# Scores, evictions and transposes in another order in a two-layer graph attention kernel on one core

## What is computed

```python
h = jnp.maximum(_layernorm(x), 0.0)
for l in range(2):
    m_left  = einsum('bsh,oh->bso', h, W_left[l]);  u_left  = einsum('bih,bjh->bij', h, m_left)  / sqrt(768)
    m_right = einsum('bsh,oh->bso', h, W_right[l]); u_right = einsum('bih,bjh->bij', h, m_right) / sqrt(768)
    u = u_left * triu(adj, 0) + u_right * swapaxes(triu(adj, 1), 1, 2)
    e = exp(u) * adj
    attention = e / (sum(e, axis=2, keepdims=True) + 1e-10)
    ctx = attention @ (einsum('bsh,oh->bso', h, W_lin[l]) + b_lin[l])
    h = relu(_layer_norm(ctx, ln_a[l], ln_b[l]))
return x + h
```

## Time and profile before

| | |
|---|---|
| median of 3 runs | 2853.18 us (2851.03 to 2854.72) |
| the profiled execution | 2853.21 us |
| its span, first to last instruction | 2851.4 us |
| TensorE matmuls busy | 2726.8 us, 96% of the span, 14400 matmuls |
| VectorE busy | 1658.9 us, 58% |
| ScalarE busy | 699.5 us, 25% |
| GpSimd busy | 109.2 us, 4% |
| DMA | 207.97 MB, mean 73 GB/s |
| mean granted TensorE clock | 0.994 |

### The profile page before, as it was taken

How to read it: one execution, slowest core, us unless ns; L and a number is a source line. 1 busy time by engine, 2 the same in 40 slices (tenths; PEclk the granted TensorE clock), 3 DMA queues, 4 the chain that set the end, 5 groups by cost and what they waited for, 6 DMA issues and landing times.

```text
span 2851.4 us, 41124 instructions
## 1 busy us (share of the span) xinstructions
PE 2726.8 (96%) x14400; PEld 2453.3 (86%) x14400; DVE 1658.9 (58%) x3394; ACT 699.5 (25%) x1131; POOL 109.2 (4%) x207
## 2 busy tenths in 40 slices
PE   5999999999999999999989999999999999999997
PEld 4888888888888888888878888888888888888886
DVE  5655566555666555655565555565555565555656
ACT  3332222232222222222232222122221122211121
POOL 0000000000000000000000000000000000000000
PEclk9999999999999999999999999999999999999998
DMA  7432223332223332233262222222221222221311
GB/s 171 103 89 82 77 69 78 77 93 82 74 62 79 88 87 80 64 79 89 52 138 51 61 61 57 59 64 58 60 58 50 70 50 61 61 62 54 72 39 57
DMA packets 574473, 207.97 MB, mean 73 GB/s; under 512 B 514272, under 2 KB 532704, under 8 KB 574432
## 3 DMA queue, kind: packets, MB, share of 16 engines
q1 hardware_dynamic: 574432, 207.43, 29.8%
HBM read 125.57 MB, written 77.59 MB: 71 GB/s over the span
## 4 chain that ended last, share of the span: by engine, by line
PE 78%; DVE 8%; SPq 5%; DMA 3%; ACT 3%; issue 2%; ACTq 0%; DVEq 0%
PE pm L580 54%; PE pm L632 14%; PE pu L620 5%; PE pc L649 5%; SPq L370 4%; DVE side L814 3%; DMA ebd<-us 2%; ACT side L709 1%; DVE turned L751 1%; DVE side L818 1%; DVE side L820 1%; DVE et L739 1%; SPq L496 1%; ACT et L716 1%; DMA vec<-in_L_gnn_W_lin_dram 0%
## 5 line engine op out<-in xcount | busy, mean ns | idle before, releaser
L580 PE MATMUL pm<-ht,wt 128*128 128x512 f32 (+1 forms) x7488 | 1616.2, 374 | 39.1 <-DVE ht L739 35.2
L580 PEld LDWEIGHTS pm<-ht,wt 128*128 128x128 f32 x7488 | 1322.4, 189 | 276.7 <-issue 29.2
L632 PE MATMUL pm<-wt,ht 128*128 128x384 f32 x4608 | 828.8, 336 | 50.8 <-DVE hl L739 45.6
L632 PEld LDWEIGHTS pm<-wt,ht 128*128 128x128 f32 x4608 | 800.7, 189 | 61.2 <-DVE hl L739 55.8
L739 DVE TENSOR_TENSOR gt<-pm,gt 128x512 fp32r<-128x512 f32 x384 | 265.2, 691 | 725.7 <-ACT gt L695 724.7
L695 ACT CAST gt<-pm 128x512 fp32r<-128x512 f32 x384 | 224.4, 584 | 1074.0 <-PE pm L580 1073.3
L739 DVE TENSOR_TENSOR hl<-pm,hl 128x384 fp32r<-128x384 f32 x256 | 141.1, 551 | 267.4 <-ACT hl L700 266.4
L700 ACT CAST hl<-pm 128x384 fp32r<-128x384 f32 x256 | 122.2, 477 | 458.5 <-PE pm L632 458.4
L620 PEld LDWEIGHTS pu<-gt,ht 128*128 128x128 f32 x1536 | 210.7, 195 | 9.6
L620 PE MATMUL pu<-gt,ht 128*128 128x256 f32 x1536 | 214.3, 282 | 0.0
L649 PE MATMUL pc<-hl,et 128*128 128x386 f32 (+1 forms) x768 | 160.6, 344 | 20.8 <-DVE et L739 18.8
(11 more groups left out here) (59 smaller groups left out, 726.0 us busy)
## 6 DMA issues: line engine op xcount, KB each, us to landing
rows<-h_dram SPq DMA_DIRECT2D x512, 96.0 KB, 3.0
side<-in_x_dram SPq DMA_DIRECT2D x126, 384.0 KB, 3.4
h_dram<-side SPq DMA_DIRECT2D x126, 384.0 KB, 2.4
out_dram<-side SPq DMA_DIRECT2D x62, 384.0 KB, 2.6
mask<-in_adj_dram SPq DMA_DIRECT2D x32, 128.0 KB, 2.5
ebd<-us SPq DMA_DIRECT2D x64, 64.0 KB, 2.4
side<-in_L_gnn_W_left_dram SPq DMA_DIRECT2D x10, 384.0 KB, 4.0
side<-in_L_gnn_W_right_dram SPq DMA_DIRECT2D x10, 384.0 KB, 4.2
```

The lines of the kernel that those rows point to most:

```text
L580: last = nc.tensor.matmul(pm[:, k % M_BANKS, t0 * P:t1 * P], wt[:, lr, a, kc, oc * P:(oc + 1) * P], ht[:, kc, t0:t1, b, :], start=(kc == 0 ...
L632: last = nc.tensor.matmul(pm[:, j % M_BANKS, 0:HALF], ht[:, kc, t, a, :], wt[:, LIN, b, kc, half * HALF:(half + 1) * HALF], start=(n == 0) ...
```

## The change

In the list of every group that has a follower, `H 1 0` stands between `U 0` and `U 1`, `TX 0` stands behind `EP`, and the weight step `v[2]`, which is empty but in the sixteenth group, behind `ET`. The last group's list is as it was.

```diff
-    steps = [("H", 0, 0), *v[0], ("H", 0, 1), ("S", 5), ("U", 0), ("U", 1), ("TX", 0), ("H", 1, 0), ("EX",), ("EM",),
-             ("EP",), ("T", 0), ("H", 1, 1), ("adj",), *v[1], ("TX", 1), ("H", 2, 0), ("T", 1), *v[2], ("ET",),
+    steps = [("H", 0, 0), *v[0], ("H", 0, 1), ("S", 5), ("U", 0), ("H", 1, 0), ("U", 1), ("EX",), ("EM",), ("EP",),
+             ("TX", 0), ("T", 0), ("H", 1, 1), ("adj",), *v[1], ("TX", 1), ("H", 2, 0), ("T", 1), ("ET",), *v[2],
              ("TX", 2), ("H", 2, 1), ("C", 0), *v[3], ("H", 3, 0), ("T", 2), ("TX", 3), *v[4], *v[5], ("T", 3),
              ("H", 3, 1), ("C", 1)]
```

## The result

The changed kernel takes 2907.11 us (median of 4 runs, 2905.43 to 2907.75), the kernel before 2852.11 us beside it (2850.87 to 2854.72): a ratio of 1.0191, 95% interval 1.0173 to 1.0208. It is slower by 55 us, where +46 was forecast. The span of its profiled execution is 2905.9 us, 54.5 longer, the mean granted clock 0.983 in place of 0.994. TensorE's matmuls count 26 us more busy time for the same 14400 matmuls (page, first part). The number of matmuls is the same, so this is the clock and not work.

The account below looks back on a forecast made before the run. TensorE was taken as the bound, its waits for half-tile evictions and et's split lengthening the end. Order +15, late rows +8, fifteenth group -3 and clock +26 gave +46 on 2853.21: 2899 us, range 2868 to 2913.

Parts of the forecast that it names:

- its wait of 1.44: TensorE before H(2,0), waiting for the eviction of H(1,0): the wait of 1.44 us was to go.
- The new wait before H(2,1): TensorE waits for the bank of H(1,1), freed later: 2.2 us where none was, bounds 1.9 and 2.5.
- The wait before the context: TensorE before the context of tile 0, waiting for the low part of et: 0.2 us left.
- The rows of tile 3: SyncE issues them later, so the first M side waits 0.6 us in 13 first-layer groups: +8 us.
- The fifteenth group: Its ebd issues go ahead of two weight loads, shortening the context's wait of 3.47: -3 us.
- The clock: Granted clock falls behind the new wait in three groups of four, costing 1.45 or 0.85 us each: +26 us.
- the order: Waits added less waits saved in an ordinary group: about +0.5 us in each of 30 groups, +15 us.
- That the clock holds: Rival: no fall of the clock behind the new waits of 2.2 us; +20, 2873 us; chance 0.2.
- five falls behind six waits: TensorE waits over 1.8 us behind its start, in the kernel before: the clock fell behind five of six.
- the one row of 2.35: The one of those six waits, 2.35 us, behind which the clock held; evidence for the held-clock rival.
- The rival of the late rows: Tile 3's rows cost 1.5 us, not 0.6, in 13 groups, every ordinary group falls: +61, 2914 us; chance 0.1.
- The faster rival: Chain to H(1,1)'s low part 2.2 us shorter, so H(2,1) and context don't wait: -58, 2795 us; chance 0.05.

Follow-up runs that it names:

- the reordered version: Changed kernel with both pairs' ScalarE copies first, H(1,1) before tile 0's split, et's before tile 1's, tile 3's rows before adjacency, two evictions before tile 2's transpose: 2794.3 us.

## Why the prediction was right, point by point

**The order decides.** All three moves did what they were said to do. H(2,0) lost its wait of 1.44, the context its own.

**The new wait before H(2,1)** was summed at 2.2 with bounds 1.9 and 2.5, and is 2.52, just over the upper bound. Two small errors, one sign. I let H(2,0) begin at the modelled end of H(1,1), but in an unbroken run the next matmul begins 0.16 ahead of that end (the context of tile 1 at 1012.08, against 1005.81 + 6.43), so TensorE was ready 0.15 earlier. And the low part of H(1,1) starts 0.99 behind that of ht, not 0.87 (2250.74 to 2251.73). The rest of the chain came out to 0.02: the pair starts 1.73 behind the cast of H(1,0) (2243.62 to 2245.35), where 1.7 was summed.

**The wait before the context**, summed at 0.2, is there though the list of waits does not show it. Without a fall H(2,1) began at 1001.16 and the context at 1004.65, 3.49 later; in an unbroken run it would have begun at 3.42 less 0.16. That is 0.23, less than the tail of the modelled end, so no idle time is recorded. For an ordinary group +0.5 was forecast; the groups without clock and queue effects show +0.64 (87.43 against 86.79). The longer new wait would add 0.3. Part of it comes back because a wait costs about 0.15 more than the profile prints as idle. In the kernel before, H(2,0) starts 7.85 behind H(1,0) (968.38 to 976.23), and two half tiles in an unbroken run take 6.27 (1005.81 to 1012.08): 1.58 lost where 1.44 is printed. The change takes away two such waits and brings one, and the sum had all three at their printed length.

**The rows of tile 3** were to cost 0.6 in 13 groups, 8 us. They cost 10.5 in eleven, 0.96 each: SyncE's issue of these rows came 2.4 later against the cast of H(1,0), not 1.8 (15.66 against 13.30). The first group, which the sum left out, waited as well (0.48). In the remaining first-layer groups of the profile a fall of the clock stood in the same place and took it over.

**The fifteenth group** was to gain 3 us, and the two groups around the change of layer gained 3.0.

**The clock** was the term with the most doubt: falls in three groups of four at 1.45 or 0.85, +26. There were falls behind 20 of 31 of the new waits in the profile, each costing 1.2 in the second layer. Both factors of the product were off there, in opposite directions: the clock fell in 15 groups of 15, not in three of four, and each fall cost 1.22, not 1.45. The price was mis-sized in two places. The fall itself lengthened the 18 matmuls by 1.57 (4.99 against 3.42), not by 1.65. And the cover is larger: besides the 0.23 before the context, the context itself took 1.21 in an unbroken run behind a fall, and 1.33 behind its wait, so 0.35 comes off and not 0.2, which leaves the 1.22. In the first layer, where falls and late rows share one place, a fall costs nothing, not 0.85, and only three ordinary groups of the profile had one. The mean granted clock came out at 0.983, not near 0.975. Of the first-layer groups the first eleven had no fall and the wait for the rows, the next three had the fall and no such wait, and nearly all of both are 88.5 to 88.8 us long.

Put together: 0.64 in 28 ordinary groups is 18 for the order (15 forecast for 30); what a first-layer group loses beyond that, late rows or fall, is 1.3, 18 in 14 groups (16 forecast); the falls of the second layer 17 (17 forecast with the first group's); -3 (-3 forecast); and 4.4 at the start and the end of the kernel, for which nothing stood in the sum. That makes 54.5 before rounding. Half of the 4.4 is ahead of the first exponential, which in the profiles here comes anywhere from 108.1 to 114.0 us, so it cannot be put down to the change.

The order, the two waits and the queue are right as mechanisms. That the terms of the clock come so close is in good part luck: more falls at a smaller price in the second layer, and in the first a wait for rows that takes the place of a fall, group by group, at nearly the same length.

**The rivals.** That the clock holds is refuted: five falls behind six waits was the better guide than the one row of 2.35. The rival of the late rows counted 30 us for falls beside waits of 1.5. By the prediction's own rule such waits would have covered the falls of the first layer, which leaves 16 x 1.45 = 23 and a sum of +54, not +61. The Trainium skill's rule on idle gaps ("TensorE: Matmul & The Clock Gate", section "Why this matters for your kernels") gives a longer gap than those behind which the clock fell here, 2.52 and also 1.78 us, and the measurement decides. The faster rival's place was the right one: with the bank of H(1,1) free in time, the reordered version comes to 64 us less, against 58 worked out there. But that version moves five more things, and the change doesn't get there by its own order.

## What to carry to other kernels

When an instruction is moved ahead of another on one engine, look at what every other engine that walks the same list does with the pair: here the gain was on VectorE, and half of the price on ScalarE, whose copies fell behind a cast that waits for TensorE; the work behind them was then all late. Order a queue by who is waited for next, and check the DMA queue in the same breath, since loads that had slack lose it when smaller ones are put ahead. A wait of 1.8 to 2.5 us on TensorE cost 1.2 more here where the clock fell and nothing covered it: count a possible fall of the clock with any new wait, and ask whether another wait behind it covers it.

## What the runs showed of the hardware that was not expected

The same wait does not always bring a fall of the granted clock. Behind waits of 2.5 us before H(2,1), at the same place in each group, the clock held in the first eleven groups and fell in the 20 after them in the first profile, and on another chip the same kernel had falls in 30 of 31 groups, from the first on. Behind waits of 1.78 us it fell in 18 of 31 groups, in no simple pattern, and behind waits of 0.97 in none. How many falls a kernel shows can so differ between profiles of one program, without a change in its waits. Here the time hardly told: the second profile has eleven falls more in the first layer, where a fall costs next to nothing, and the ratios are 1.0191 and 1.0186.
